# Packing the edge records' index fields as words on VectorE, loading the edge attributes into eight buffers, and weighting ten of sixteen blocks on GpSimd

## The reference, cut to what matters

```python
sc = jax.nn.softplus(deg_coeff[0] * deg_v + deg_coeff[1])   # deg_v: one value per edge
base = adj_v * sc * (row != col)                            # adj_v: one value per edge
...
alpha = x_i @ wa[:c] + edge_attr @ wa[c:c + ce] + x_j @ wa[c + ce:]   # edge_attr: 16 per edge
```

## Time and profile before

| | us |
|---|---|
| median of 3 runs | 3576.33 (3574.14 to 3576.89) |
| the profiled execution | 3570.82 |
| its span | 3568.7 |
| last store of REC issued | 139.59 |
| busy PE, DVE, ACT, POOL | 2903.2, 2851.9, 2211.9, 1535.5 |
| mean granted TensorE clock, share of full speed | 0.939 |

### The profile page before, as it was taken

The page is one execution under the profiler, slowest core; times in us unless marked ns, Lnnn a source line. Parts: engine busy times, 40 slices in busy tenths (PEclk is TensorE's granted clock), DMA queues, the critical chain, the costliest instruction groups (busy, mean ns, idle before and its releaser), DMA issues.

```text
span 3568.7 us, 121778 instructions
## 1 busy us (share of the span) xinstructions
PE 2903.2 (81%) x50424; PEld 2637.3 (74%) x50424; DVE 2851.9 (80%) x4608; ACT 2211.9 (62%) x5954; POOL 1535.5 (43%) x1099
## 2 busy tenths in 40 slices
PE   0199999999999599899688887787766888888886
PEld 0078888888888599898677777777766777777775
DVE  7599999999999623233588878988856999998996
ACT  6334444444444400001598988898866999998897
POOL 2012222222221170000298988998981444444444
PEclk9999999999999899999899999999986988898887
DMA  8157777777777799899687877787747888888884
GB/s 222 67 157 243 238 234 235 237 243 237 232 235 241 241 377 363 331 329 329 220 277 256 273 250 251 258 271 245 265 146 250 309 287 281 288 303 278 279 297 133
DMA packets 614265, 910.48 MB, mean 255 GB/s; under 512 B 361305, under 2 KB 502460, under 8 KB 594765
## 3 DMA queue, kind: packets, MB, share of 16 engines
q1 hardware_dynamic: 591594, 803.69, 68.6%
q10 hardware_dynamic: 19763, 94.38, 7.2%
q0 software_dynamic: 2352, 4.52, 0.3%
HBM read 653.81 MB, written 248.63 MB: 253 GB/s over the span
## 4 chain that ended last, share of the span: by engine, by line
PE 38%; DVE 23%; ACT 15%; issue 10%; DMA 7%; POOL 7%; ACTq 1%; SPq 0%; DVEq 0%; POOLq 0%
PE ps L684 8%; PE ps L1078 8%; PE ps L710 4%; DMA U<-AD 4%; ACT U L1682 4%; POOL EDG L1300 3%; PE ps L697 3%; ACT U L570 2%; DVE U L1849 2%; POOL EDG L1292 2%; DMA EDG<-ROWS 2%; ACT U L1361 2%; PE ps L1321 2%; PE ps L1718 2%; PE ps L668 1%
## 5 line engine op out<-in xcount | busy, mean ns | idle before, releaser
L570 ACT ACTIVATE U<-ps 128x512 bf16<-128x512 f32 (+1 forms) x637 | 356.3, 573 | 498.1 <-PE ps L697 474.3
L1682 ACT ACTIVATE U<-U,T 128x65 f32<-128x65 f32 x1806 | 460.3, 343 | 44.7 <-PE ps L1728 42.8
L1695 POOL TENSOR_TENSOR U<-U 128x455 f32<-128x455 f32 x258 | 304.2, 1181 | 350.6 <-DVE U L1849 350.6
L1078 PE MATMUL ps<-U 128*128 128x192 bf16 x4802 | 416.3, 247 | 37.8 <-DMA U<-AD 37.7
L1078 PEld LDWEIGHTS ps<-U 128*128 128x128 bf16 x4802 | 401.7, 98 | 45.9 <-DMA U<-AD 43.0
L1292 POOL TENSOR_TENSOR EDG<-U,edge 128x512 f32<-128x512 f32 (+1 forms) x196 | 214.1, 1097 | 499.1 <-DVE edge L1444 465.0
L867 DVE TENSOR_TENSOR EDG<-edge,EDG 128x1792 bf16<-128x1792 bf16 x343 | 368.6, 1087 | 14.8 <-DMA OSD<-EDG 14.1
L684 PE MATMUL ps<-U 128*128 128x98 bf16 (+1 forms) x5292 | 363.3, 223 | 4.1 <-DVE U L855 3.6
L503 POOL DMA_INDIRECT U<-REC,nod x49 | 94.4, 1926 | 614.5 <-PE ps L639 493.5
L710 PE MATMUL ps<-EDG,U 128*128 128x193 bf16 x2401 | 311.9, 249 | 50.6 <-ACT U L570 39.7
L684 PEld LDWEIGHTS ps<-U 128*128 128x128 bf16 x5292 | 341.0, 98 | 14.1 <-DVE U L855 8.0
(11 more groups left out here) (322 smaller groups left out, 7040.3 us busy)
## 6 DMA issues: line engine op xcount, KB each, us to landing
U<-ROWS SPq DMA_DIRECT2D x411, 448.0 KB, 4.7
U<-AD SPq DMA_DIRECT2D x98, 1568.0 KB, 8.7
OND<-EDG SPq DMA_DIRECT2D x343, 224.0 KB, 2.8
OSD<-EDG SPq DMA_DIRECT2D x343, 224.0 KB, 3.6
AD<-U ACTq DMA_DIRECT2D x49, 1568.0 KB
EDG<-ROWS SPq DMA_DIRECT2D x171, 448.0 KB, 6.3
U<-OND SPq DMA_DIRECT2D x303, 224.0 KB, 6.0
U<-OSD SPq DMA_DIRECT2D x213, 224.0 KB, 4.8
```

The costliest lines, as they stand in the source:

```text
L570: ev4.by(act.activation(prow[i % NPW][:, P * g:P * (g + m)], ps[4 + gg % 2][:, 0:P * m], ACT.Copy))
L1078: ins = pe.matmul(ps[q][:, 0:192], arow[r][:, P * j:P * j + P], (XsB if p else XsA)[:, j, :, :].rearrange("p s f -> p (s f)"), start=(j == ...
L1682: ins = act.activation(V4[k % NV][:, 0, c, :], H[k % NHR][:, c, :], ACT.Copy, scale=a4[d % 2][:, s:s + 1])
L1695: look.by(pool.tensor_tensor(V4[k % NV][:, 2, :, :], V4[k % NV][:, 1, :, :], S4[k % NV][:, 1, :, :], ALU.subtract))
```

## The change

- The attributes have eight buffers (NEB = 8): six in E3 as before, one in the upper half of A, one in the upper half of T. GpSimd no longer clears E3. ScalarE's queue gets the load of `war` and then the first eight blocks at once; blocks 8 to 15 are issued by SP.
- The other 17 parameter loads move to SP's queue, behind the four edge planes. `x` is loaded by SP after the last attribute block. The stores of REC move from SP to ScalarE (`stored`).
- GpSimd multiplies the blocks of POOLED by the weights; VectorE keeps six blocks, for which it holds the 16 weights in PSUM (`wrow`), and all sums.
- Fields 0 to 3 are no longer written one by one by ScalarE into RB. ScalarE turns them into floats in dense tiles; VectorE shifts the two lower ones right by 16 bits and writes each pair as one 32-bit word (RW is RB seen as words).
- VectorE does blocks 0 and 1 first, and the arguments of ScalarE's activations come ahead of the counting. Five semaphores are used a second time instead of having new ones.

```diff
+        RW = part(4 * C, KB * NF * 16).bitcast(I32).rearrange("p (k w) -> p k w", w=NF // 2)
-        KE, NEB = 98, 6
+        KE, NEB = 98, 8
+        eab = [e.rearrange("p (k f) -> p k f", f=16) for e in
+               [e3flat[:, 16 * KE * n:16 * KE * (n + 1)] for n in range(6)] + [Aflat[:, C:2 * C], Tflat[:, C:2 * C]]]
+        POOLED = (2, 3, 4, 5, 7, 8, 10, 11, 13, 14)
+        wrow = ps[6][:, 0:16]
...
         def head_sp(sp):
...
+                ld_par.by(sp.dma_start(dstap, srcap), 16)
+            sp.wait_ge(pad_dst.at, 2)
+            for b in range(NEB, NEA):
+                sp.wait_ge(ea_used.at, b - NEB + 1)
+                attributes_loaded(sp, b)
+                if b == NEB + 1:
+                    sp.wait_ge(filled.at, 3)
+                    rec_st.by(sp.dma_start(REC[NK:NK + 4 * CH, :].rearrange("r f -> (r f)").rearrange("(p k) -> p k", p=P), fill), 16)
+                    sp.wait_ge(ld_edges.at, 96)
+                    for f, plane in ((0, srci), (1, dsti)):
+                        side_st.by(sp.dma_start(ENDS[f].rearrange("(p k) -> p k", k=C), plane), 16)
...
+        def head_act(act):
+            war_ld.by(act.dma_start(war[:, :], watt[0, :].partition_broadcast(P)), 16)
             for b in range(NEB):
-                attributes(b)
+                if b == 6:
+                    act.wait_ge(filled.at, 2)
+                attributes_loaded(act, b)
+            act.wait_ge(ints.at, 1)
+            field_a.by(act.activation(dstf, it[1], ACT.Copy))
+            for i in (0, 2, 3):
+                field_a.by(act.activation(it[i].bitcast(F32), it[i], ACT.Relu, bias=1.0))
...
+            pool.wait_ge(war_ld.at, 16)
+            for b in POOLED:
+                n = EBLOCKS[b][1]
+                pool.wait_ge(ea_ld[b % NEB].at, attribute_loads(b))
+                weighted.by(pool.tensor_tensor(eab[b % NEB][:, 0:n, :], eab[b % NEB][:, 0:n, :],
+                                               bc(war[:, 64:80].unsqueeze(1), [P, n, 16]), ALU.mult))
...
         def head_dve(dve):
...
+            def attributes(b):
+                k0, n = EBLOCKS[b]
+                i = b % NEB
+                if b in POOLED:
+                    dve.wait_ge(weighted.at, POOLED.index(b) + 1)
+                else:
+                    dve.wait_ge(ea_ld[i].at, attribute_loads(b))
+                    dv.by(dve.tensor_tensor(eab[i][:, 0:n, :], eab[i][:, 0:n, :], bc(wrow.unsqueeze(1), [P, n, 16]), ALU.mult))
+                    dve.wait_ge(dv.at, dv.n)
+                ea_used.by(dve.tensor_reduce(ea[:, k0:k0 + n], eab[i][:, 0:n, :], AX, ALU.add))
+            for b in range(2):
+                attributes(b)
             dve.wait_ge(ld_edges.at, 96)
...
+            dve.wait_ge(ld_par.at, 16 * 17)
...
-            for b in range(NEB):
+            for b in range(2, 7):
                 attributes(b)
...
+            dve.wait_ge(field_a.at, 4)
+            for f, i in ((0, 0), (1, 2)):
+                dv.by(dve.tensor_scalar(it[i], it[i], 16, None, ALU.logical_shift_right))
+            dve.wait_ge(dv.at, dv.n)
+            for f, low, high in ((0, it[0], dstf.bitcast(I32)), (1, it[2], it[3])):
+                packed.by(dve.tensor_tensor(RW[:, :, f], low, high, ALU.bitwise_or))
+            for b in range(7, 9):
+                attributes(b)
```

More of the change, by code:

```diff
@@ L177, in gnn_kernel, with attribute_loads, attributes_loaded @@
         ea_ld = [sem(f"ea_ld{i}") for i in range(NEB)]
+        war_ld, weighted, packed = sem("war_ld"), sem("attribute_weighted"), sem("fields_packed")
         def rows_of(d):
             return d[0:(P - 1) * C].rearrange("(p k) -> p k", k=C), d[(P - 1) * C:E].rearrange("(p k) -> p k", p=1)
+        def attribute_loads(b):
+            return 16 * sum(3 if LASTE > EBLOCKS[r][0] else 2 for r in range(b % NEB, b + 1, NEB))
+        def attributes_loaded(eng, b):
+            k0, n = EBLOCKS[b]
+            i = b % NEB
+            for p0, p1 in ((0, 112), (112, P - 1)):
+                ea_ld[i].by(eng.dma_start(
+                    eab[i][p0:p1, 0:n, :], eattr[p0 * C:p1 * C, :].rearrange("(p k) f -> p k f", k=C)[:, k0:k0 + n, :]), 16)
+            nl = max(0, min(n, LASTE - k0))
+            if nl:
+                ea_ld[i].by(eng.dma_start(
+                    eab[i][P - 1:P, 0:nl, :],
+                    eattr[(P - 1) * C + k0:(P - 1) * C + k0 + nl, :].rearrange("(p k) f -> p k f", p=1)), 16)
         def head_sp(sp):
@@ L194, in head_sp @@
                 ld_w.by(sp.dma_start(tile[P - 1:P, 0:LASTE], last), 16)
[L195 to L214, removed]
             for dstap, srcap in ((sc[:, 0:2], dcoef.partition_broadcast(P)), (sc[:, 2:5], cpar.partition_broadcast(P)),
-                                 (sc[:, 5:6], spar.partition_broadcast(P)), (war[:, :], watt[0, :].partition_broadcast(P)),
+                                 (sc[:, 5:6], spar.partition_broadcast(P)),
                                  (Wst[0:D, :], W1n), (Wst[D:P, :], W1r),
@@ L254, in head_act @@
             arg_out.by(act.activation(base, base, ACT.Ln, bias=1.0))
[L255 to L262, removed]
             def attribute_field(q, m):
@@ L271, in attribute_field, with stored @@
                 att_a.by(act.activation(RB[:, c0:c1, 5 + 2 * m], (rem[1] if m else ea)[:, c0:c1], ACT.Copy))
+            def stored(q):
+                b0, b1 = RUNS[q]
+                act.wait_ge(field_a.at, 7)
+                act.wait_ge(packed.at, packed.o + 2)
+                act.wait_ge(att_a.at, 3 * q + 3)
+                rec_st.by(act.dma_start(REC[0:NK, :].rearrange("(p b) f -> p b f", p=P)[:, b0:b1, :],
+                                        RB.rearrange("p (b e) f -> p b (e f)", e=32)[:, b0:b1, :]), 16)
+            act.wait_ge(split_in.at, 1)
+            field_a.by(act.activation(RB[:, :, 4], base, ACT.Copy))
             attribute_field(0, 0)
@@ L320, in head_dve @@
             pad_dst.by(dve.memset(X[:, NB - 1, :], 0.0))
+            def attributes(b):
+                k0, n = EBLOCKS[b]
+                i = b % NEB
+                if b in POOLED:
[5 more added lines that the diff above has]
+                ea_used.by(dve.tensor_reduce(ea[:, k0:k0 + n], eab[i][:, 0:n, :], AX, ALU.add))
+            dve.wait_ge(war_ld.at, 16)
+            dv.by(dve.tensor_copy(wrow, war[:, 64:80]))
+            dve.wait_ge(dv.at, dv.n)
+            for b in range(2):
+                attributes(b)
             dve.wait_ge(ld_edges.at, 96)
@@ L403, in head_dve @@
             attribute_rest(0, 0)
-            for b in range(8, 11):
-                attributes(b)
+            attributes(9)
             dve.wait_ge(field_a.at, 6)
@@ L409, in head_dve @@
             attribute_rest(0, 1)
+            attributes(10)
             attribute_rest(1, 0)
-            for b in range(11, 13):
-                attributes(b)
+            attributes(11)
             attribute_rest(1, 1)
+            attributes(12)
             attribute_rest(2, 0)
-            for b in range(13, NEA):
+            for b in range(13, 15):
                 attributes(b)
             attribute_rest(2, 1)
+            attributes(15)
             attribute_rest(3, 0)
@@ L628, in pairs_act @@
                 act.wait_ge(rw_st[r].at, rw_st[r].n)
-            act.wait_ge(root_in.at, 1)
+            act.wait_ge(root_in.at, root_in.o + 1)
             root_out.by(act.activation(nod[:, 0, :], nod[:, 1, :], ACT.Sqrt))
```

66 lines of the change are left out of this document (23 added, 43 removed).

## The result

The changed kernel takes 3580.14 us (median of 20 runs, 3571.57 to 3590.82), the kernel before in the same measurement 3573.93 us (20 runs, 3568.35 to 3583.84). The ratio is **1.002, 95% interval 1.0011 to 1.0028**: slower by about 7 us (4 to 10).

What follows compares the result with a forecast made beforehand. The head, alternating ScalarE and VectorE, was taken to go one to one into the span: front part +23.1 us, later part 11.6 us gained, sum +11.5, so 3587.8 us; range 3567 to 3600 us.

Steps and rivals of the forecast that it cites:

- Parameters at about 50 us: Head, SP's queue: small parameter packets alternate with large attribute packets, landing at about 50 us (45 to 53), leaving VectorE idle.
- Rival 1: Head's loads: parameters get through early, at about 36 us; +4.6 us, 3581 us, the same; chance 0.12.
- L371's place at 61.2 us, blocks 2 to 6 by 71.8: VectorE after the parameters: reaches operations up to L371 at 61.2 us instead of 34.15, blocks 2 to 6 by 71.8.
- Four turns on VectorE: VectorE around base and the shifts: four GpSimd multiplications each hold it once, 0.6, 3.2, 3.2 and 3.2, together 10.2 us.
- Rival 2: Head: GpSimd does not hold VectorE, parameters still at 50 us; +1.3 us, 3578 us, the same; chance 0.12.
- Words 3.0 us each: VectorE's two ORs writing 4 bytes to a 20-byte step: 3.0 us each, its price for reading at that step.
- Rival 4: VectorE's ORs are dear, 7.2 us each: +20 us, 3596 us; within the forecast's own range, no separate chance given.
- L434 ends at 103.7 us, then 47.4 us to the last store: Head: L434 ends 23.1 us later than before; from there to the last REC store 47.4 us instead of 59.0.
- Last store at 151.1 us, +11.5: End of the head: last REC store issued at 151.1 us instead of 139.6, going one to one into the span.
- 3587.8 us: Whole kernel: profiled execution 3570.8 us plus 11.5 gives 3582.3; the median shown is 5.5 us above it.
- Rival 3: Head: parameters before about 42 us, GpSimd's work in VectorE's waits and reductions, no idle stretch; -15 us, 3562 us; chance 0.16.
- The change's first idea: ScalarE's four field copies in the head, now dense: 4 x 1.5 instead of 4 x 7.2 us, lying in VectorE's wait.

Runs made afterwards that it cites:

- experiment 3: Changed kernel with the 17 parameter loads on ScalarE's queue behind attribute blocks 0 and 1; last REC store issued at 153.75 us against 149.42.
- experiment 4: Changed kernel with the 17 parameter loads first on SP's queue, ahead of the edge planes; last REC store issued at 145.96 us.
- experiment 1: Changed kernel, but GpSimd begins block 10 only after VectorE's first remainder of base; 3568.26 us against 3572.52 for the kernel before, ratio 0.9995.
- experiment 5: Kernel before with one part alone: packed fields (last REC store 139.59 us, as before), or 18 parameter loads on SP behind the planes (head 1.4 us longer).
- experiment 7: Changed kernel with VectorE's three first-needed parameters loaded ahead of ScalarE's attribute blocks, others awaited after block 6, GpSimd not delayed; last REC store at 138.52 us.
- experiment 6: On top of experiment 1, VectorE's three first-needed parameters loaded ahead of the attribute blocks; 3555.89 us against 3572.52 for the kernel before, ratio 0.9963.
- experiment 8: On top of experiment 6, blocks 7 and 8 summed behind the first remainder of base; 3549.97 us against 3568.9 for the kernel before, ratio 0.9947.
- experiment 9: Multiplications read weights from SBUF, not PSUM: in the changed kernel, last REC store 147.81 us; in the kernel of experiment 8, store 2.13 us later.

## Why the prediction was right, step by step

- *Parameters at about 50 us (45 to 53), by turns of packets:* 47.42 us, and 50.39 us in another execution with the same loads. Experiments 3 and 4 show the turns with other partners. The rule in the Trainium skill (DMA: Bandwidth & Descriptors, Queues, rings and completion order) of switches at packet boundaries fits; its 9 to 17 descriptors per packet do not, if a descriptor is a row: the turns seen from 32.34 us on are of about one row each. Rival 1 fell with it.
- *L371's place at 61.2 us, blocks 2 to 6 by 71.8:* 61.68 and 71.98 us, partly by luck. The parameters came 2.6 us sooner, and the cast L370, which I had not counted among the operations that GpSimd can hold, took 3.3 us more.
- *Four turns on VectorE, 10.2 us, 3.2 us by GpSimd's time for 1,568 values:* 10.1 us (0.43 + 3.17 + 3.30 + 3.17 over 1.78 us each), and experiment 1 takes them away. GpSimd alone takes 3.48 us; the estimate of 3.4 us from the Trainium skill (GPSIMD Engine Reference, Performance versus the Vector engine) was the closer one. Their places were half wrong: all four were on base, none at the shifts, since GpSimd was done at 87.4 us and the holds themselves had pushed the shifts to 89 us. That all four cost the same wherever they fall made the sum come out. A fifth hold, of one of the first shifts (L358, 4.26 us at 22.44 us), was not in the prediction and lay in VectorE's wait for the parameters. Rival 2 fell.
- *Words 3.0 us each, as the engine's reads at that step:* 3.01 and 3.00 us. Rival 4 fell.
- *L434 ends at 103.7 us, then 47.4 us to the last store:* 102.87 us and 46.55 us.
- *Last store at 151.1 us, +11.5:* 149.42 us, +9.83.
- *3587.8 us:* 7.7 us above the measured median. 1.7 us are the head. 2.4 us are the median of before, 3573.93 us in the larger set and 3576.33 in the three runs that I had added the change to. The other 3.6 us are between the head's +9.8 and the medians' +6.2; the interval of the ratio (4 to 10 us) holds both.
- *Rival 3, faster, if the parameters came before 42 us:* its place was right and its condition was not enough. In experiment 3 they came at 40.06 us, and the head was longer than in the changed kernel, since they had delayed GpSimd's blocks to where VectorE's small operations stand. In experiment 7 they were there at 27 us, and the head is only 1.1 us shorter than before. It took GpSimd's later start too: experiments 6 and 8 end the head 13.7 and 17.1 us sooner than before.
- *The change's first idea* had no price in the prediction's sum, and experiment 5 shows it: packed fields alone move nothing.

## What to carry to other kernels

Making an engine's slow work faster is worth nothing while its own stream waits for someone else; look at what ScalarE's next useful instruction waits for before making its copies faster. A wait should ask only for what the next instruction reads: three tiny loads of seventeen were needed at 27 us, and splitting the wait gave back 10 to 13 us. When a second engine does its work is decided by the loads that feed it; tie its start to a point where the first engine waits anyway, or the two hold each other.

## What the runs showed of the hardware that I had not expected

- The hold between VectorE and GpSimd goes by whole instructions and both ways. A GpSimd multiplication (3.48 us alone) took 5.98 us in experiment 1, with VectorE's comparison started 0.04 us ahead. On VectorE the size does not matter: a cast of 49 elements per partition went from 0.20 to 3.49 us and an operation on 3 elements from 0.23 to 3.29. One input is no protection either (the shifts, 0.97 to 4.28 us). Sums over blocks (L348) were never held, at most 1.80 us, nor multiplications of blocks with their weights in PSUM, at most 1.81 us; with the weights in SBUF one took 2.68 us (experiment 9).
- Two queues take turns by packets even when one has 4 to 12 bytes in most of its packets and the other 6,272. Meanwhile SP spent up to 6.3 us on one issue of a 32 KB parameter (L225 at 33.76 us), where the issue before it, also 32 KB, took 0.43.
- A start a little earlier or later decided over 3.3 us of the head: GpSimd 0.15 us ahead of the cast in the changed kernel (49.13 against 49.28 us), VectorE 0.27 us ahead in experiment 1, with the same code and loads up to there. The 3.0 us between the two executions of experiment 1 have another cause, the parameters 2.9 us later.
